# The decayed input of the chunk states, made by ScalarE one head at a time instead of by VectorE in one operation

## The reference, cut to what matters

```python
xch = (hs * dt[..., None]).reshape(b, nc, CHUNK, H, P)
Y_diag = einsum('bzlhn,bzshn,bhzls,bzshp->bzlhp', Cc, Bc, L, xch)
decay_states = exp(A_cum[..., -1:] - A_cum)
states = einsum('bzlhn,bhzl,bzlhp->bzhpn', Bc, decay_states, xch)
...
Y_off = einsum('bzlhn,bzhpn,bhzl->bzlhp', Cc, prev, exp(A_cum))
Y = (Y_diag + Y_off).reshape(b, s, H, P) + hs * D[None, None, :, None]
g = Y.reshape(b, s, INTER) * silu(gate)      # then a group norm and the output projection
```

## Time and profile before

| what | us |
|---|---|
| median of 3 runs (lowest, highest) | 1657.9 (1655.18, 1663.19) |
| profiled execution, its own time | 1656.76 |
| span of the profile, first to last instruction | 1654.6 |
| TensorE matmuls in flight | 1616.8 |
| VectorE busy | 1367.3 |
| GpSimd busy | 1341.1 |
| ScalarE busy | 1232.1 |

### The profile page before, as it was taken

One profiled execution on the slowest core, in us unless ns is written; L12 is line 12 of the kernel. 1 busy time (PEld: TensorE's weight loads), 2 busy tenths in 40 slices (PEclk: granted clock), 3 DMA queues, 4 the chain that ended last, 5 costly groups with the idle time before them and its releaser, 6 DMA issues.

```text
span 1654.6 us, 31655 instructions
## 1 busy us (share of the span) xinstructions
PE 1616.8 (98%) x10792; PEld 1300.1 (79%) x10792; DVE 1367.3 (83%) x1675; ACT 1232.1 (74%) x2625; POOL 1341.1 (81%) x1238
## 2 busy tenths in 40 slices
PE   7999999999999999999999999999999999999998
PEld 6777878878787877878778787887878787787776
DVE  5979788887979878788888888888788887879787
ACT  5267787777877777777877778687786877778775
POOL 3148689886998779897798968988698977989797
PEclk9999999999999999999999999999999999999999
DMA  3253366553644545454554535535454365544463
GB/s 129 68 190 112 101 186 178 152 155 109 197 127 123 151 154 163 112 149 128 166 176 116 157 115 166 164 115 164 125 183 125 115 170 141 158 127 146 127 164 104
DMA packets 216399, 236.09 MB, mean 143 GB/s; under 512 B 154280, under 2 KB 155824, under 8 KB 212016
## 3 DMA queue, kind: packets, MB, share of 16 engines
q1 hardware_dynamic: 216240, 234.08, 47.7%
HBM read 147.52 MB, written 55.05 MB: 122 GB/s over the span
## 4 chain that ended last, share of the span: by engine, by line
PE 65%; POOL 13%; ACT 8%; DVE 7%; issue 6%; DMA 0%; ACTq 0%; DVEq 0%; POOLq 0%; SPq 0%
PE P L261 8%; PE P L263 8%; PE P L262 8%; PE P L470 5%; PE P L480 5%; PE P L345 4%; PE P L487 4%; PE P L339 4%; PE P L338 4%; PE P L481 4%; ACT P L583 4%; PE P L495 3%; DVE hsX L790 2%; POOL xch L1115 2%; POOL AL L1090 2%
## 5 line engine op out<-in xcount | busy, mean ns | idle before, releaser
L583 ACT ACTIVATE P<-AB,SC 128x128 f32<-128x128 f32 x1016 | 305.9, 364 | 0.0
L261 PE MATMUL P<-xh,AH 128*128 128x512 f32 x656 | 267.8, 408 | 2.6 <-DVE xl L891 1.8
L790 DVE SCALAR_TENSOR_TENSOR hsX<-P,cwt,hsX 128x1023 f32<-128x1023 f32 x189 | 241.9, 1280 | 25.7 <-ACT hsX L520 21.2
L263 PE MATMUL P<-xh,AL 128*128 128x512 f32 x656 | 257.1, 392 | 0.0
L262 PE MATMUL P<-xl,AH 128*128 128x512 f32 x656 | 255.5, 389 | 0.0
L755 ACT ACTIVATE sq<-yb 128x512 bf16<-128x512 f32 x128 | 80.8, 631 | 212.6 <-DVE yb L1054 212.6
L1090 POOL TENSOR_TENSOR AL<-AR,AH 128x512 fp32r<-128x512 f32 x82 | 116.1, 1416 | 133.5 <-ACT AH L507 133.4
L480 PE MATMUL P<-OH,gTh 128*128 128x512 f32 x512 | 214.6, 419 | 2.5 <-DVE hsX L1070 1.5
L338 PE MATMUL P<-GH,xh 128*128 128x512 f32 x512 | 200.1, 391 | 0.2 <-ACT GH L552 0.2
L481 PE MATMUL P<-OH,gTl 128*128 128x512 f32 x512 | 200.3, 391 | 0.0
L339 PE MATMUL P<-GH,xl 128*128 128x512 f32 x512 | 199.6, 390 | 0.0
(11 more groups left out here) (214 smaller groups left out, 4144.2 us busy)
## 6 DMA issues: line engine op xcount, KB each, us to landing
AB<-acr_d SPq DMA_DIRECT2D x128, 512.0 KB, 4.6
half_d<-hsX SPq DMA_DIRECT2D x60, 512.0 KB, 3.3
AR<-in_wa SPq DMA_DIRECT2D x80, 256.0 KB, 2.8
TS<-in_wg SPq DMA_DIRECT2D x16, 1024.0 KB, 5.8
TS<-in_wo SPq DMA_DIRECT2D x16, 1024.0 KB, 4.8
part_d<-pl SPq DMA_DIRECT2D x64, 256.0 KB, 3.1
pl<-part_d SPq DMA_DIRECT2D x64, 256.0 KB, 3.2
SC<-sct_d SPq DMA_DIRECT2D x16, 128.0 KB, 5.3
```

Source lines behind the costliest of these rows:

```text
L261: te.matmul(o, ah_, bh_, start=(first and i == 0), stop=False)
L263: r = te.matmul(o, al_, bh_, start=False, stop=(last and i == n - 1))
L583: r = se.activation(decays(m)[:, h, :], AB[m % 2][:, h, :], ACT.Relu, bias=SC[s % 2][:, c, 3, h:h + 1], scale=-1.0)
L790: ve.scalar_tensor_tensor(out=o[:, d:T], in0=raw[:, 0:T - d], scalar=cwt[:, n, 3 - d:4 - d], in1=o[:, d:T], op0=ALU.mult, op1=ALU.add).the ...
```

## The change

The multiplication leaves VectorE's queue. ScalarE makes the same tile with eight operations, one for each head: a copy of 64 columns with a scale from memory, one number for each token. They stand in `act_state_hi`, behind the high part of `S` and ahead of the high part of `dxh`. The waits that VectorE had for the tile go along: for the rows `HT`, for the scales `SC` and for GpSimd's last reading of `dxh` (`s_dl`); a wait for ScalarE's own last reading (`s_dh`) is new. The last chunk of a group, in which VectorE waited for `HT` without making anything, has no such wait any more. Nothing else changes place.

```diff
+        def act_scaled(m):
+            s, c = divmod(m, 8)
+            if s:
+                se.wait_ge(ht_in[m % 2], 16 * (m // 2 - 3))
+            else:
+                se.wait_ge(s_hsr, m + 1)
+            se.wait_ge(sc_in[s % 2], 32 * (s // 2 + 1))
+            if m:
+                se.wait_ge(s_dl, n7(m) - 1)
+                se.wait_ge(s_dh, n7(m) - 1)
+            for h in range(8):
+                d = slice(h * 64, h * 64 + 64)
+                r = se.activation(dxh[:, d], HT[m % 2][:, d], ACT.Copy, scale=SC[s % 2][:, c, 2, h:h + 1])
+            r.then_inc(s_dxh, 1)
+
         def act_state_hi(m):
...
             if m % 8 != 7:
+                act_scaled(m)
                 se.wait_ge(s_dxh, n7(m))
...
-        def dve_scaled(m):
-            s, c = divmod(m, 8)
-            if s:
-                ve.wait_ge(ht_in[m % 2], 16 * (m // 2 - 3))
-            else:
-                ve.wait_ge(s_hsr, m + 1)
-            ve.wait_ge(sc_in[s % 2], 32 * (s // 2 + 1))
-            if c != 7:
-                if m:
-                    ve.wait_ge(s_dl, n7(m) - 1)
-                ve.tensor_tensor(h8(dxh[:, :]), h8(HT[m % 2]), bc(SC[s % 2][:, c, 2, :]), ALU.mult).then_inc(s_dxh, 1)
...
             dve_blocks(0)
-            dve_scaled(0)
             dve_decay(0)
...
                         dve_output_lo(s, (0,))
-                    dve_scaled(m + 1)
```

## The result

The change makes the kernel 0.8% slower: the median of four runs is 1671.91 us (1670.47 to 1674.01) against 1657.35 us of the kernel before on the same chip (four runs). The ratio is 1.0083, with a 95% interval of 1.0055 to 1.0111. 1680 was predicted, with a range of 1664 to 1696. The profiled execution took 1672.36 us itself, 15.6 above that of before, and its span is 1671.1 us, 16.5 above.

What follows compares the result with a forecast made beforehand. TensorE's queue was taken to set the time, with ScalarE's slack chunk by chunk deciding the change. Odd starts 13.3, even starts 6.3, group 0 2 and the end 1 sum to 22.6 us over the median: 1680, range 1664 to 1696.

Steps and rivals of the forecast that it cites:

- The length of the new operations: ScalarE's eight operations a chunk: each some 0.33 us long, 0.25 apart, 2.0 us of queue a time.
- Only the first two chunks of the groups pay: Main loop: losses fall in the groups' first two chunks; middle chunks, with waits of 2.7 or more, cost nothing.
- ScalarE's wait before the square: ScalarE's wait for the gated rows, whole kernel: expected to fall from 207 to below 80 us.
- A wait for the decayed input at the state product: Sign of being wrong: a wait for L602 or L1127 showing up at the state product.
- The price of 90 us: Whole kernel, by the rule alone: 0.8 us in each of 112 moves; not used in the sum.
- Start of an odd group: First two chunks of groups 1 to 13: ScalarE's lateness costs 1.25 then 0.65, 1.9 a group, 13.3 us.
- the last rival: Group starts and ends: late L1127 delays state and add, 1.5 us more per pair of groups; 1688 to 1700, chance 0.14.
- Start of an even group: First two chunks of groups 2 to 14: 0.5 through GpSimd's queue, then 0.4; 0.9 a group, 6.3 us.
- less 0.2 for operations that VectorE's multiplication no longer slows: First chunk of even groups: a give-back taken off GpSimd's 0.7 us delay, leaving 0.5.
- the relieved-GpSimd rival: 14 group starts and 7 chunks of group 15: 0.45 each comes back, 9.5 us; about 1649, chance 0.06.
- Ends: Group 0's first two chunks cost some 2 us; group 15 and three chunks of group 14 cost 1 us.
- ScalarE becomes the bound: At 3.0 us a time further chunks are late too, 46 us; about 1704, chance 0.08.

Runs made afterwards that it cites:

- experiment 4: The kernel before, with ScalarE making the decayed input only in chunks 3 to 6 of each group and chunk 0 of even groups from 2 on: 1652.82 us, ratio 0.9963.
- experiment 7: The kernel before without VectorE's multiplication (decayed input not made), with eight spare ScalarE copies behind the high part of the decayed input: 1666.95 us, ratio 1.0056.
- experiment 3: The kernel before without VectorE's multiplication and nothing put on ScalarE instead, so the decayed input is not made: 1641.78 us, ratio 0.9901.
- experiment 1: The kernel before, VectorE's multiplication kept, plus eight spare 64-column ScalarE copies ahead of the high part of the decayed input: 1673.54 us, ratio 1.0089.
- experiments 2: The kernel before, VectorE's multiplication kept, plus eight spare 64-column ScalarE copies behind the high part of the decayed input: 1673.55 us, ratio 1.0088.
- experiment 6: The changed kernel with four spare ScalarE copies more behind its eight operations: 1706.21 us, ratio 1.0298 against the kernel before.
- experiment 8: The kernel before, ScalarE making the tile in chunks 3 to 6, chunk 0 of even groups from 2, half the heads in chunk 2 (group 15 all): 1650.86 us.

## Why the prediction was right

The time lies 8 us under the 1680 forecast and within the range. The steps at the starts and ends held to 4 us of 22.6; the rest of the difference are gains that weren't foreseen.

**The length of the new operations: right.** 0.25 apart and 0.33 long were forecast from the relus. Eight take 2.01 us with 0.337 for one, so they start (2.01 - 0.337) / 7 = 0.239 apart.

**Only the first two chunks of the groups pay: right**, but for 0.17 in the chunk ahead of each odd group, and the middle chunks keep their length, by the table and by experiment 4. TensorE's wait for the gated rows rose by 11.6 us as forecast, all of it in those two chunks. ScalarE's wait before the square was to fall below 80 us and fell to 90.1. A wait for the decayed input at the state product, a sign of being wrong, stayed at next to nothing: 1.4 us. The price of 90 us, 0.8 us in each of 112 moves, stood beside the rule of the Trainium skill that gives multiplications to VectorE ("ScalarE: Activation LUTs", Rules for kernel authors); it was an estimate from this kernel's rows. The direction was that of the rule; the size was 14.6, because most of the moved time stands in ScalarE's idle time.

**Start of an odd group: 1.9 forecast, 1.76 measured** (0.17 + 0.73 + 0.86, the 0.17 in the chunk ahead), with two errors against each other. ScalarE of the kernel after in order of time, through the start of group 9:

```profile
1020.10 2.01 ACT L602 ACTIVATE dxh<-hsX,SC 128x64 f32<-128x64 f32 x8
1022.14 0.63 ACT L618 ACTIVATE DH<-dxh 128x512 fp32r<-128x512 f32 x1
...
1023.16 0.62 ACT L771 ACTIVATE sq<-yb 128x512 bf16<-128x512 f32 x1
...
1031.00 1.01 ACT L588 ACTIVATE P<-P 128x1024 f32<-128x1024 f32 x1
...
1035.64 0.61 ACT L771 ACTIVATE sq<-yb 128x512 bf16<-128x512 f32 x1
...
1037.61 1.06 ACT L547 ACTIVATE hsX<-hsX 128x1024 uint16<-128x1024 uint16 x1 [0.30 <-DVE hsX L835]
...
1047.42 0.63 ACT L771 ACTIVATE sq<-yb 128x512 bf16<-128x512 f32 x1 [0.67 <-DVE yb L1056]
```

VectorE, in order of time:

```profile
1032.10 1.23 DVE L864 TENSOR_TENSOR EM<-P,Gt 128x1024 f32<-128x1024 f32 x1 [1.78 <-issue]
...
1035.24 2.34 DVE L835 SCALAR_TENSOR_TENSOR hsX<-th,hsX 128x1024 f32<-128x1024 f32 x1
...
1042.14 3.92 DVE L806 SCALAR_TENSOR_TENSOR hsX<-P,cwt,hsX 128x1023 f32<-128x1023 f32 x3 [1.52 <-ACT hsX L520]
```

GpSimd:

```profile
1035.20 1.30 POOL L1129 TENSOR_TENSOR DL<-dxh,DH 128x512 fp32r<-128x512 f32 x1 [0.82 <-ACT DH L618]
1036.46 2.04 POOL L1132 TENSOR_TENSOR S<-S,EA 128x512 f32<-128x512 f32 x1
```

TensorE:

```profile
1034.81 0.63 PE L495 MATMUL P<-ident,yb 128*128 128x128 f32 x4 [0.80 <-DVE yb L1056]
...
1047.54 0.63 PE L495 MATMUL P<-ident,yb 128*128 128x128 f32 x4 [0.90 <-DVE yb L1056]
```

The square at 1023.16 has no wait left where it had 0.46; VectorE's decay product starts 0.1 after the exponential ends (1032.01), as forecast; and TensorE waits 0.80 for the rows that it used to turn without a wait. That is the step as written, with 0.8 where 1.25 stood. In the second chunk the tap is late and the convolution behind it waits 1.52. TensorE waits 0.90 (0.36 before), and of the 2.72 ahead of the next square 0.67 are left. There the sum was too low, 0.65 against 0.86. The silu at 1035.24 takes 2.34 us, against 1.47 in the same place before:

```profile
1025.68 1.47 DVE L819 SCALAR_TENSOR_TENSOR hsX<-th,hsX 128x1024 f32<-128x1024 f32 x1
...
1024.78 1.29 POOL L1127 TENSOR_TENSOR DL<-dxh,DH 128x512 fp32r<-128x512 f32 x1
1026.02 2.05 POOL L1130 TENSOR_TENSOR S<-S,EA 128x512 f32<-128x512 f32 x1
```

The product with the state's decay behind the low part took its 2.05 before as it does after, against 1.06 in other places. What is new is the low part: it waited 0.82 for its high part, and 1.26 us of it lie beside the silu where 0.39 did, which is the 0.87 by which the silu is longer. ScalarE's L547 waits for the end of that silu. I had the low part's lateness in the last rival, as a delay of the state. It came as contention, with the state product untouched. Without the late low part (experiment 7) the silu still takes 2.04 and the chunk loses 0.56, near the 0.65 of the sum; the other 0.30 are what it is worth.

**Start of an even group: 0.9 forecast, 0.64 measured.** The second chunk came as forecast (0.4, measured 0.49); the first cost 0.15 and not 0.5. The term "less 0.2 for operations that VectorE's multiplication no longer slows" was mis-sized: what GpSimd gets back in these two operations is 0.9. GpSimd's two low parts, each 1.74 before, in group 10 of the kernel after:

```profile
1124.03 1.29 POOL L1206 TENSOR_TENSOR OL<-TS,OH 128x512 fp32r<-128x512 f32 x1
1126.18 1.30 POOL L1092 TENSOR_TENSOR AL<-AR,AH 128x512 fp32r<-128x512 f32 x1 [0.86 <-ACT AH L507]
...
1124.39 1.47 DVE L829 SCALAR_TENSOR_TENSOR OL<-TS,nwt,OH 128x512 fp32r<-128x512 f32 x1 [0.29 <-ACT OH L789]
```

0.45 + 0.44 are given back, and the wait of 0.86 for ScalarE's rounding takes them again. GpSimd's 0.54 from the chunk ahead (experiment 3) is there too, and goes to a wait of 0.62 for the late high part of the decayed input. So the mechanism of the relieved-GpSimd rival was there, but the prediction read one of its two rows wrongly: the 1.74 at 918.33 needs no multiplication, as experiment 3 shows. VectorE's low part of the output weights had started first (917.43), the multiplication only at 918.84. In the change that VectorE operation waits for ScalarE and starts 0.36 behind GpSimd's (1124.39), which takes 1.29. Experiment 3 shows what the whole relief is worth with nothing put on ScalarE, 15.7 us. What the rival lacked was the rounding in time.

**Ends: 3 forecast, 1.8 measured** (1.6 in group 0, 0.8 in group 14's last chunk, -0.6 in group 15).

**Not foreseen:** 0.38 back in the last three chunks of each odd group (7 x 0.38 = 2.6 us; experiment 3 has the same, so it is relief), the first gated rows 1.1 earlier, 0.9 less outside the span, and the clock's 1.6 at the end. By the two profiled executions' own times 22.6 us were forecast and 1672.36 - 1656.76 = 15.6 came. The 7.0 between them: 1.0 at the odd starts, 1.8 at the even ones, 1.2 at the ends, 2.6 + 1.1 + 0.9 not foreseen, less 1.6. The 1.1 is relief too. Of the kernel before, in VectorE's queue ahead of the first gated rows (121.22), in which nothing behind 117.98 waits:

```profile
118.97 1.00 DVE L848 TENSOR_TENSOR dxh<-hsX,SC 128x512 f32<-128x512 f32 x1
```

The four kernels in which this multiplication is gone have their first gated rows at 119.9 to 120.4; the six that keep it, or half of it, at 121.2 or later.

**Why load and relief don't add.** This is a reading of the runs, and no run takes the two ways apart at one start. What each does at a start goes to the same gated rows by two ways: through ScalarE's queue (square, exponential, tap) and through VectorE's and GpSimd's (product with the decay, low parts, add). The rows are made when the later way is done. Before, the two end close to each other at a start: the first made longer costs at once (+16), and the second made shorter gains at once (-15.7). Make the first longer, and the second has slack that nobody uses: the relief falls to 6.8 (experiment 7) and, with the decayed input itself late, to 1.5 (the change against experiment 1, 16.05 - 14.56), which can't be told from nothing. Where the 6.8 stand fits this: by the chunks of experiments 2 and 7 most of them are away from the starts, 2.6 in the last chunks of the odd groups, 1.6 in group 15 and 2.1 ahead of the first gated rows (1.0 of it the clock, below), where the load costs little or nothing; an odd start keeps 0.1 of its relief of 0.3, an even one 0.2 of 1.0. With VectorE's whole multiplication taken away, 0 us of queue give -15.7, 2.0 give +14.6 and 2.9 give +48.5, so the last 0.9 cost more than the first 2.0. With half of it taken away and 1.0 us of queue the kernel is 5 us faster.

The rival "ScalarE becomes the bound", priced at 1704 for 3.0 us a time, found its test in experiment 6: 1706.2 for 2.87 us. It was priced by lateness in 7 further chunks in 16. Experiment 6 puts it elsewhere: nearly all in the first two and the last chunk of the groups, at 0.5 to 1.4 each. And its sum was off: its 46 us are what comes on top of the starts as they were counted, but were added to 1658 without the 22.6 of these, and "the four above at one more each" went in as 3. So the total was right by luck.

**Left open.** It wasn't tried to put the new operations behind the square in ScalarE's queue, where their first followers would be less urgent.

## What to carry to other kernels

Before work is moved to an engine with idle time, list that engine's waits chunk by chunk: what the move adds costs nothing up to the wait that follows it, and what goes past the wait is paid in part or in full (1.2 or 0.8 us a group here for 2.0 us in each of 7 chunks; of 0.87 us more in each, 0.8 came back as lost time in the first two and the last chunk of the even groups). Then move it only there, or move only as much as the shortest wait holds: both beat the kernel before. Price what the relieved engine's neighbours gain apart from what the loaded engine loses, and take the later of the two ways at each join, not the sum.

## What the runs showed of the hardware

- VectorE and GpSimd slow each other by far more than I had assumed, and not always both: beside the silu of 2.34 us GpSimd's low part kept its 1.30, and its product with the state's decay took 2.04. VectorE's multiplication (128x512) took between 0.68 and 1.78 us in the kernel before, 0.68 in all 18 places with little or nothing of GpSimd beside it, and its silu (128x1024) between 1.21 and 2.37 in the kernel after. The rows read as if the one that starts second got on only when the other was done: GpSimd's low part ends at 1036.50 (1035.20 + 1.30), and the silu that began 0.04 behind it ends 1.08 later, where 1.21 is its length alone. The rows of experiments 3 and 7 above read the same way, but no run here was made to test it. That the two share their SBUF interfaces is what the "GPSIMD Engine Reference" of the Trainium skill states (section Specifications); the sizes are those of these rows. And half of the columns don't take half of the time: alone, a half multiplication took 0.41 us against 0.68, but of those of experiment 8 one at the start of group 8 took 1.51, more than many whole ones.

```profile
916.33 1.51 DVE L882 TENSOR_TENSOR dxh<-hsX,SC 128x256 f32<-128x256 f32 x1
```

- TensorE's clock can fall at the end of a kernel, after some 2 us with little for it to do: 0.57 in the last output product of the change (above), 1.00 at the same place of the kernel before, after the same pauses. It can fall near the start as well: between 16 and 21 us it was 0.66 in experiments 1, 2 and 8, whose first gated rows come 2.1, 0.9 and 1.3 later than those of the kernel before, and 1.00 in the kernels before and after. VectorE's queue is 2.1, 1.0 and 1.4 late at 38 us already, before any operation that these kernels add.
